# Attention scores of a two-layer transformer from two exact parts of q and k in the rounded four-byte type, one 32-row tile of TensorE per head, instead of three bf16 parts in 64-row tiles

## The reference

```python
q = jnp.einsum('bnc,hc->bnh', x, Wq).reshape(b, n, m, d)      # n = 1024, m = 16 heads, d = 8
k = jnp.einsum('bnc,hc->bnh', x, Wk).reshape(b, n, m, d)
v = jnp.einsum('bnc,hc->bnh', x, Wv).reshape(b, n, m, d)
scale = d ** (-0.25)
weight = jnp.einsum('bimd,bjmd->bmij', q * scale, k * scale)
weight = jax.nn.softmax(weight, axis=-1)
a = jnp.einsum('bmij,bjmd->bimd', weight, v).reshape(b, n, m * d)
return jnp.einsum('bnh,ch->bnc', a, Wout) + bout
```

## Time and profile before

| what | us | share of the span |
|---|---|---|
| median of three runs | 2011.02 | |
| profiled execution | 2013.06 | |
| its span | 2011.7 | |
| TensorE busy | 1826.9 | 91% |
| VectorE busy | 1521.9 | 76% |
| ScalarE busy | 1373.9 | 68% |
| GpSimd busy | 740.5 | 37% |
| weight loads of TensorE | 735.0 | 37% |
| DMA of hardware queue q1 | | 15.6% of 16 engines |

### The profile page before, as it was taken

The page is one execution under the profiler, slowest core; times in us unless marked ns, Lnnn a source line. Parts: engine busy times, 40 slices in busy tenths (PEclk is TensorE's granted clock), DMA queues, the critical chain, the costliest instruction groups (busy, mean ns, idle before and its releaser), DMA issues.

```text
span 2011.7 us, 39958 instructions
## 1 busy us (share of the span) xinstructions
PE 1826.9 (91%) x15950; PEld 735.0 (37%) x15950; DVE 1521.9 (76%) x2326; ACT 1373.9 (68%) x1826; POOL 740.5 (37%) x1150
## 2 busy tenths in 40 slices
PE   6675799999999999999999999999999999999994
PEld 4552333333433343343433344343433334222222
DVE  5456777888777877878777877778778787899961
ACT  2431467776687767777677766877677776887883
POOL 1441353315633265323744155332653145102001
PEclk9886799999999999999999999999999999999996
DMA  2012021012111121102211121111311021111101
GB/s 61 31 46 81 23 73 51 29 42 80 39 52 31 53 84 55 48 6 83 72 51 31 40 85 36 50 31 53 94 51 31 15 79 56 53 45 46 32 16 37
DMA packets 97258, 99.36 MB, mean 49 GB/s; under 512 B 11088, under 2 KB 81456, under 8 KB 97072
## 3 DMA queue, kind: packets, MB, share of 16 engines
q1 hardware_dynamic: 95224, 94.84, 15.6%
q10 hardware_dynamic: 1848, 1.97, 0.3%
HBM read 61.25 MB, written 34.73 MB: 48 GB/s over the span
## 4 chain that ended last, share of the span: by engine, by line
PE 63%; ACT 14%; DVE 11%; issue 5%; POOL 4%; DMA 1%; SPq 1%; ACTq 0%; POOLq 0%; DVEq 0%
PE pv_psum L667 18%; PE buffer L651 9%; PE buffer L641 9%; ACT p L846 9%; DVE row_max L1071 7%; PE side_psum L442 4%; PE side_psum L517 3%; PE side_psum L565 3%; PE side_psum L570 3%; PE side_psum L523 2%; PE side_psum L540 2%; PE side_psum L533 2%; PE side_psum L490 2%; PE side_psum L576 1%; POOL hm L1190 1%
## 5 line engine op out<-in xcount | busy, mean ns | idle before, releaser
L1071 DVE TENSOR_REDUCE row_max<-buffer 128x2 f32<-128x1024 f32 x1024 | 1239.6, 1221 | 319.5 <-PE buffer L641 305.9
L846 ACT ACTIVATE p<-buffer 128x1024 f32<-128x1024 f32 x1024 | 1044.0, 1025 | 283.5 <-PE buffer L651 265.0
L667 PE MATMUL pv_psum<-p,v 128*9 128x256 f32 x8192 | 638.6, 384 | 5.3 <-ACT o_sb L852 2.4
L641 PE MATMUL buffer<-k_ops,q_ops 48*128 48x512 bf16 x2048 | 398.8, 387 | 59.6 <-ACT p L846 23.1
L651 PE MATMUL buffer<-q_ops,k_ops 51*128 51x512 bf16 x2048 | 401.1, 388 | 18.7 <-DVE row_max L1071 15.3
L667 PEld LDWEIGHTS pv_psum<-p,v 128*9 128x9 f32 x8192 | 121.6, 88 | 350.4 <-issue 325.8
L651 PEld LDWEIGHTS buffer<-q_ops,k_ops 51*128 51x128 bf16 x2048 | 98.2, 93 | 343.5 <-DVE row_max L1071 155.6
L1203 POOL TENSOR_SCALAR nm_parts<-nm 128x16 bf16<-128x16 f32 x64 | 13.3, 208 | 413.2 <-DVE nm L1020 412.2
L641 PEld LDWEIGHTS buffer<-k_ops,q_ops 48*128 48x128 bf16 x2048 | 99.7, 94 | 178.9 <-ACT p L846 139.0
L1190 POOL TENSOR_TENSOR hm<-masks,hT_f 128x1024 f32<-128x1024 bf16 x64 | 136.6, 2146 | 39.5 <-PE side_psum L570 34.9
L1167 POOL TENSOR_TENSOR s<-s,consts 128x128 f32<-128x128 f32 x64 | 29.3, 458 | 242.5 <-ACT s L763 242.5
(11 more groups left out here) (245 smaller groups left out, 1873.5 us busy)
## 6 DMA issues: line engine op xcount, KB each, us to landing
masks<-masks_rows SPq DMA_DIRECT2D x16, 1024.0 KB, 5.6
q_ops<-products SPq DMA_DIRECT2D x128, 96.0 KB
k_ops<-products SPq DMA_DIRECT2D x124, 96.0 KB
products<-q_parts SPq DMA_DIRECT2D x16, 384.0 KB, 2.6
products<-k_parts SPq DMA_DIRECT2D x14, 384.0 KB, 2.9
attention<-o_sb SPq DMA_DIRECT2D x256, 18.0 KB
x<-in_L_attn_inputs SPq DMA_DIRECT2D x8, 512.0 KB, 4.0
products<-q_parts SPq DMA_DIRECT2D x16, 256.0 KB, 3.1
```

Source lines behind the costliest of these rows:

```text
L641: m = e.matmul(buffer[:, hh, :], q_ops[rows_of(hh, K_MAX), slot, of, i * P:(i + 1) * P], k_ops[rows_of(hh, K_MAX), slot, of, halves(half)[ ...
L667: m = e.matmul(pv_psum[q:q + VW, half * QUARTER:(half + 1) * QUARTER], v1[b % 2][:, kb, 2 * hp + hh, :], p_sb[n % 4][:, hh, part * QUARTER ...
L846: e.activation(p_sb[n % 4][:, :, :], unit("exp", n)[0][:, :, :], ACT.Exp).then_inc(S["exp_done"], 1)
L1071: e.tensor_reduce(mx[pair % 2][:, :, i, half], unit("max", n)[0][:, :, :], axis=AX.X, op=ALU.max).then_inc(S["max_done"], 1)
```

## The change

Two type and layout changes go together.

1. q, k and the maxima are split into **two** parts in float32r (`F32R`: four bytes, mantissa rounded) instead of three in bf16. Three products are stacked: 24 rows (`K_MAX`), 26 with the two parts of the maximum (`K_EXP`). All tiles and the DRAM buffer of the operands become float32. Score matmuls read them as float32r.
2. A head gets **32** rows of the array (`ROW_TILE`). The exp scores read partitions 0 to 63, the max scores partitions 64 to 127, so each half's four score matmuls lie in four different row tiles. The same rows are therefore fetched twice, once for `max` 43 halves ahead and once for `exp` 11 halves ahead, for one pair at a time, into two slots each.

With them go: ScalarE's copy of the first part (L802) and two of GpSimd's four instructions on the maxima; one of the three instructions of a split of q or k; a memset of `k_ops` of another shape; the transposition of the maxima in float32. The three bf16 parts of the experts' bias stay (`BE_PARTS`). The planner and its tables are not touched.

```diff
-PARTS = 3
-Q_PART = (0, 0, 0, 1, 1, 2)
-K_PART = (0, 1, 2, 0, 1, 0)
+BE_PARTS = 3
+PARTS = 2
+Q_PART = (0, 0, 1)
+K_PART = (0, 1, 0)
...
-ROW_HALF = 64
-GROUP = 2
-GROUPS = HEADS // 2 // GROUP
-SLOTS = 3
+ROW_TILE = 32
+SLOTS = 2
...
-    q_ops = sb("q_ops", [P, SLOTS, GROUP, N], BF16)
-    k_ops = sb("k_ops", [P, SLOTS, GROUP, N], BF16)
+    q_ops = sb("q_ops", [P, SLOTS, N])
+    k_ops = sb("k_ops", [P, SLOTS, N])
...
+    def fetch_operands(queue, kind, pair, w):
+        b, hp = divmod(pair, HEADS // 2)
+        for hh in range(2):
+            head = DH * (2 * hp + hh)
+            queue.dma_start((q_ops, k_ops)[w][rows_of(kind, hh, K_MAX), pair % SLOTS, :],
+                            products_dram[b % 2, w, :, head:head + DH, :]).then_inc(operands(kind, pair)[0], 16)
+
+    def rows_of(kind, hh, count):
+        first = ROW_TILE * (hh if kind == "exp" else 2 + hh)
+        return slice(first, first + count)
...
         def exp_scores(n):
...
+            pe.wait_ge(*operands("exp", pair))
             pe.wait_ge(*maxima_in(pair))
             for hh in range(2):
-                m = e.matmul(buffer[:, hh, :], k_ops[rows_of(hh, K_EXP), slot, of, kb * P:(kb + 1) * P],
-                             q_ops[rows_of(hh, K_EXP), slot, of, halves(half)[1]], start=True, stop=True)
+                m = e.matmul(buffer[:, hh, :], k_ops[rows_of("exp", hh, K_EXP), slot, kb * P:(kb + 1) * P].bitcast(F32R),
+                             q_ops[rows_of("exp", hh, K_EXP), slot, halves(half)[1]].bitcast(F32R), start=True, stop=True)
...
         def qk1(b, w, half):
             v, cols = filled("qk1", b, w, half), halves(half)[1]
-            act.wait_ge(S[f"parts{w}"], 16 * STORES * b)
-            e.copy(qk1_parts[w][:, 0, cols], v)
...
-        for hh in range(2):
-            e.memset(k_ops[ROW_HALF * hh + 32:ROW_HALF * (hh + 1), :, :, :], 1.0).then_inc(S["operands_set"], 1)
+        for slot in range(SLOTS):
+            e.memset(k_ops[0:2 * ROW_TILE, slot, :], 1.0).then_inc(S["operands_set"], 1)
...
-            after(e.tensor_tensor(r, r, p[:, 0, :], op=ALU.subtract))
-            after(e.tensor_scalar(p[:, 1, :], r, 1.0, 0.0, ALU.mult, ALU.add))
-            e.tensor_tensor(p[:, 2, :], r, p[:, 1, :], op=ALU.subtract).then_inc(S[f"split{w}_{half}"], 1)
+            pool.wait_ge(S[f"parts{w}"], 16 * STORES * b)
+            after(e.tensor_scalar(p[:, 0, :].bitcast(F32R), q, 1.0, 0.0, ALU.mult, ALU.add))
+            e.tensor_tensor(p[:, 1, :].bitcast(F32R), q, p[:, 0, :], op=ALU.subtract).then_inc(S[f"split{w}_{half}"], 1)
...
+        def load_operands(kind, pair):
+            sp.wait_ge(S["operands_set"], SLOTS)
+            if pair >= SLOTS:
+                sp.wait_ge(S[f"{kind}_filled"], UNITS * (pair - SLOTS + 1))
...
+            for kind, lead in (("max", 2 * LEAD), ("exp", 0)):
+                pair, within = divmod(h + lead + LOAD_BEFORE, UNITS)
+                if within == 0 and pair < PAIRS and (kind, pair) != ("max", 0) and pair >= 0:
+                    load_operands(kind, pair)
```

More of the change, by code:

```diff
@@ L6 @@
 BF16 = mybir.dt.bfloat16
+F32R = mybir.dt.float32r
 U32 = mybir.dt.uint32
@@ L336, in build @@
     mx = [sb(f"row_max{i}", [P, 2, T, HALVES]) for i in range(2)]
-    nm, nm_r = sb("nm", [P, 2, T]), sb("nm_r", [P, 2, T])
-    nm_parts = sb("nm_parts", [P, 2, PARTS, T], BF16)
-    nm_rows = [sb(f"nm_rows{i}", [PARTS * 2 * T, P], BF16) for i in range(2)]
+    nm = sb("nm", [P, 2, T])
+    nm_parts = sb("nm_parts", [P, 2, PARTS, T])
+    nm_rows = [sb(f"nm_rows{i}", [PARTS * 2 * T, P]) for i in range(2)]
     o_sb = sb("o_sb", [P, BANK])
@@ L384, in loaded, with operands @@
         return S[f"in_x{b % 4}"], 16 * (b // 4 + 1)
-    def operands(g):
-        return S[f"operands{g % SLOTS}"], 4 * GROUP * 16 * (g // SLOTS + 1)
+    def operands(kind, pair):
+        return S[f"{kind}_operands{pair % SLOTS}"], 4 * 16 * (pair // SLOTS + 1)
     def maxima_in(pair):
@@ L411, in store_parts @@
             queue.dma_start(dst, src).then_inc(S[f"parts{w}"], 16)
-    def fetch_operands(queue, g, w):
-        b, slot, p0 = g // GROUPS, g % SLOTS, (g % GROUPS) * GROUP
-        for of in range(GROUP):
-            for hh in range(2):
-                head = DH * (2 * (p0 + of) + hh)
-                queue.dma_start((q_ops, k_ops)[w][rows_of(hh, K_MAX), slot, of, :],
-                                products_dram[b % 2, w, :, head:head + DH, :]).then_inc(S[f"operands{slot}"], 16)
-    def rows_of(hh, count):
-        return slice(ROW_HALF * hh, ROW_HALF * hh + count)
+    def fetch_operands(queue, kind, pair, w):
[7 more added lines that the diff above has]
+        return slice(first, first + count)
     def tensor_program():
@@ L636, in max_scores @@
             pair, i, half = n // (2 * T), n // 2 % T, n % 2
-            slot, of = pair // GROUP % SLOTS, pair % GROUP
-            buffer = buffer_of("max", n)
-            pe.wait_ge(*operands(pair // GROUP))
+            slot, buffer = pair % SLOTS, buffer_of("max", n)
+            pe.wait_ge(*operands("max", pair))
             for hh in range(2):
-                m = e.matmul(buffer[:, hh, :], q_ops[rows_of(hh, K_MAX), slot, of, i * P:(i + 1) * P],
-                             k_ops[rows_of(hh, K_MAX), slot, of, halves(half)[1]], start=True, stop=True)
+                m = e.matmul(buffer[:, hh, :], q_ops[rows_of("max", hh, K_MAX), slot, i * P:(i + 1) * P].bitcast(F32R),
+                             k_ops[rows_of("max", hh, K_MAX), slot, halves(half)[1]].bitcast(F32R), start=True, stop=True)
             m.then_inc(S["max_filled"], 1)
@@ L1290, in sync_program @@
         sp.wait_ge(S["be_split"], 1)
-        for j in range(PARTS):
+        for j in range(BE_PARTS):
             e.dma_start(be3[j * EXPERTS:(j + 1) * EXPERTS, :], be_parts[:, j, :]).then_inc(S["be3_in"], 16)
@@ L1298, in parts @@
             if b >= 2:
-                for g in range((b - 1) * GROUPS - GROUPS, (b - 1) * GROUPS):
-                    sp.wait_ge(*operands(g))
+                for pair in range((b - 1) * HEADS // 2 - SLOTS, (b - 1) * HEADS // 2):
+                    sp.wait_ge(*operands("max", pair))
+                    sp.wait_ge(*operands("exp", pair))
             store_parts(e, b, w, half)
```

79 lines of the change are left out of this document (34 added, 45 removed).

## The result

The changed kernel takes 2087.74 us (median of four runs, 2081.48 to 2089.49) against 2011.05 (2006.14 to 2013.58) for the kernel before: ratio 1.0379, 95% interval 1.0350 to 1.0408, or 76 us more. The forecast was 1978, with a range up to 2045; the time lies outside it. The profiled execution took 2089.5 us, with a span of 2087.8, at a mean granted clock of 0.923; before it was 0.965.

The account below looks back on a forecast made before the run. Each half was taken as bound by TensorE's chain or, where it waits, ScalarE's exponential. 2013 - 70 (overlap) + 51 (weight loads) - 8 (casts) - 6 (start) = 1980, less 2 from profile to median: 1978 us, range 1915 to 2045.

Parts of the forecast that it names:

- The type's term: Float32r weight load exposed in each of 1024 halves, +50 ns over bf16: 51 us more, ends 0 and 105.
- The doubled loads: Operand loads on SP's queue double from 252 to 504 DMAs, hidden by a lead of 11 halves: costed at nothing.
- a wait of either scores for an operand DMA inside the loop: Sign that would refute costing the doubled operand loads at nothing.
- The overlap: Four score matmuls stream together, 0.215 us less in halves that don't wait: 70 us off of a 128 us ceiling.
- The rule of the waiting halves: Max scores start no earlier than 1.56 us after the previous exp scores, so waiting halves hand back their predecessor's saving.
- two cycles a column: Rival: float32r score matmuls stream at half rate, max scores to values 0.52 us; say 2140 us, chance 0.12.
- Waits for ScalarE: Max scores' waits for ScalarE's exponential rise from 398 and 139 us to some 550 times and over 250 us.
- The rest: ScalarE's casts of L802 gone, 8 us off; a shorter start, 6 us off; GpSimd, maxima and VectorE's memsets nothing.
- The load is the two-instruction one: Rival: float32r weight load costs 103 ns more instead of 50, 105 us in all; 2034 us, chance 0.12.
- No overlap: Rival: exp and max scores don't stream together, or the max scores' load cancels it; 2005 to 2020 us, chance 0.07.
- the f32 rate: Rival: score matmuls stream 512 columns in 0.95 us instead of 0.213; near 2680 us, chance 0.04.
- under 0.97 in the middle, since the array is then less busy than before: Sign: a granted clock this low in the middle of the loop would refute a term costed at nothing.

Follow-up runs that it names:

- loads_apart: The changed kernel with the exp scores' operand loads issued 15 halves ahead instead of 11: 2046.94 us, ratio 1.0180 to the kernel before.
- apart_stacked: loads_apart with both kinds of scores reading the same 56 rows per head, in two 64-row tiles instead of four: 2080.58 us, ratio 1.0340.
- bf16_apart_stacked: bf16_apart with both kinds of scores reading the same 56 rows per head, in two 64-row tiles instead of four: 1989.64 us, ratio 0.9878.
- The fillers: Zero-weight bf16 matmuls behind the values of halves without side stage, added to the changed kernel (2078.28 us) and to loads_apart (2045.29 us).
- bf16_tiles: The changed kernel with its two parts in bf16 instead of float32r, for operands, parts and maxima: 1965.24 us, ratio 0.9772.
- bf16_apart: bf16_tiles with the exp scores' operand loads issued 15 halves ahead instead of 11: 1956.43 us, ratio 0.9734.

## Why the prediction was wrong

Its sum was 2013 - 70 + 51 - 8 - 6 + 0, less 2 us between profile and median. By the table the same terms are -32, +92, -25 and +40 us. Two steps failed, the load's size and the queue at nothing, and a third thing had no term at all: the time at the lower clock.

**The type's term, 51 us: about 92.** The load was taken as that of a transposition, 50 ns over bf16. It reads 189 and 193 ns in the profile after, 96 to 100 over the bf16 loads of the earlier trace rows, and changing the type alone costs 90 and 93 us. In the halves at full clock in both traces of a pair that is 84 ns a half with four tiles and 90 with two. The step that failed is "I take the one-instruction four-byte load". The prediction's own mark was "93 or 196 moves the sum by 51 us down or 54 up", and it read nearly 196. The Trainium skill's rule that was cited (TensorE: Matmul & The Clock Gate, section Weight-path perf modes) has the fast load for types other than FP32 and doesn't place float32r; the trace places it with FP32, 189 and 193 ns against 196 for f32 and 91 to 94 for bf16. Counting it once for each half was right: 0.11 us more per half whether or not it waits.

**The doubled loads, 0 us: 40.** The failing step is "I cost it at nothing; what hides it is the lead of 11 halves". The lead was compared with one transfer, while what mattered was the small DMA of the maxima behind eight loads in the same queue. The lead did hold for the operands, since no score waits for a `products` load inside the loop, but seven times it did not for the maxima. The listed mark, "a wait of either scores for an operand DMA inside the loop", came true. That the maxima are "needed 10 and more halves later" was wrong already for the kernel before: once in a sequence they stood some 9 us in SP's queue and landed less than 1 us ahead of use, and its view of the waits shows two such waits, 1.3 us in all. Nor does "each of the same size" make two loads equal: the traces show about six of sixteen DMA engines at work for loads before and about three after. In the loop the 39 us are 16 us of waits and 22 us of lower clock behind them, net of what loads_apart has elsewhere. With half the bytes all is worth 8.

**The overlap, 70 us off: 32.** That four tiles stream together is shown: 429 of the 898 halves at full clock have their max scores less than 0.02 us behind the exp scores. The rule of the waiting halves was also right in size. In halves at full clock in both traces of a pair, the four tiles take 69 us off with float32r (967 halves) and 61 with bf16 (952). Where it comes from differs by type. With bf16, exp to max scores loses 68 us and max scores to values gains 8. With float32r it is 136 and 71: with a common start the second load has no stream to hide behind, so 0.11 us moves from one interval to the other. What was missing is the clock: loads_apart has 104 us at the low level in the loop against 14 in apart_stacked, and 30 us of the 69 are lost there; with bf16 it is 126 against 18, and 31 of the 61. The marks of the prediction read accordingly: exp to max scores under 0.03 held; max scores to values of 0.31 to 0.36 holds for bf16 (0.31 where undelayed) and not for float32r (0.42 to 0.43); 0.52, two cycles a column, is refuted.

**Waits for ScalarE** were to rise from 398 and 139 us to 550 and over 250. They fell to 291 and 113.8; a longer TensorE half leaves ScalarE more time, which is argued and not tested alone. With bf16 and the loads apart, four tiles instead of two make the matching figures 389 times and 171 us against 389 and 141, and the waits booked on the matmuls themselves 171 and 57 against 80 and 22: the argument was right in direction for a load that costs little.

**The rest, 14 us off: 25.** Casts, start, VectorE and ScalarE work, and one product part fewer. In the traces of the kernel before and bf16_apart_stacked it is 15 us in the loop, nearly all between the values and the next exp scores, and 8 us ahead of the first exp scores. The loop was costed at 8 us. The start isn't resolved by one profile: the first max scores stood at 169.4 us before and at 153.8 to 167.4 in the profiles of the kernels with two parts, and two of them with the same code for the start differ by 6.7 us. In the changed kernel the store of the k parts took 7.87 us and the first operands 7.78, against 6.35 and 6.91 in the earlier trace rows, and the first max scores came 2 us earlier than before, not 6.

**The rivals.** "The load is the two-instruction one" had 2034 us and named the right load. The 54 us between it and the measured time are the overlap (+38), the loads in the queue (+40), the rest (-11), and a type's term of 92 instead of 105 (-13). No rival had the queue or the clock. No overlap, two cycles a column and the f32 rate are refuted.

**The clock.** The mark "under 0.97 in the middle, since the array is then less busy than before" came true in part (0.98 and 0.91 in the first two stretches of the earlier trace rows), but it had no price in the sum. The price is 55 us of the change's 74 in the loop (section on the result), 0.33 us for each microsecond at the low level, in halves that were at full clock before. It isn't a fifth term beside the four of the table: each of them is measured with its share of it, above all the tiles (30 us) and the queue (22 us). At full clock throughout, the change would have cost some 20 us, an estimate: 76 less 55. The fillers agree: they gain 0.28 and 0.31 us for each microsecond that they lift to full clock, and lose 21 and 24 us by their own work. Two things stay open. Why the kernel with four row tiles falls to the low level in loads_apart, where no DMA wait starts it, no run shows. And a lower clock doesn't decide alone: bf16_tiles has 142 us of it in the loop, more than the 104 of loads_apart, and is 82 us faster.

**The better version.** bf16_apart, at 0.9734, beats both kernels, at the price of scores with fewer bits than float32. With float32r, the loads apart are the better form of the change, but still 1.8% slower than before.

## What to carry to other kernels

Before a type is changed, ask what its weight load costs and whether that load is exposed: here 100 ns on a load outweighed a stream that vanished, since an overlap that merges two starts also exposes the second load, and since the four tiles came with more time at the lower clock. Where loads are split or doubled, look for the smallest and latest DMA behind them in the same queue and compare the lead with its landing, not with theirs; a short wait of that kind in the trace before, here 1.3 us, says that the lead is used up. A gain in one interval of a loop is measured over the whole loop, by the sum of every interval; here 150 us became 32. To price a lower clock, compare the same halves at both levels in two traces; halves with different work mislead.

## What the runs showed of the hardware

- Float32r matmuls stream 512 columns in nearly the time of bf16: with the second load hidden (apart_stacked) max scores to values is 0.32 us against 0.31, and with it exposed 0.42 against 0.31, about the difference of the loads. By the Trainium skill, page FP8 and Floating Point Precision, section TensorE Precision Notes, true FP32 takes four passes through the array, while a reduced-precision FP32 is read as four bytes and truncated; the trace agrees with one pass for it.
- A float32r load of 128 columns takes 0.18 us at full clock and 0.28 at 1.2 GHz, for 24, 26 and for 56 rows nearly alike (189 and 193, 183 and 187 ns in the mean), where bf16 takes 91 to 94.
- Four row tiles on four PSUM banks start within 0.01 us of each other, for both types.
- 8 KB behind eight loads of 96 KB landed 8.87 us after its issue. While such loads, and at most stores of parts beside them, were under way, 0.38 of the sixteen DMA engines were busy with six products along the load's first dimension and 0.19 with three.
- After 3.93 us of idle time in the loop, TensorE stayed at the 1.2 GHz level for 68 us although the profile has it busy without a gap; with filler matmuls the same wait was followed by 10 us of it, and with two row tiles instead of four a wait of 4.06 us by 7.
- The same 34 halves took 65.8 us at 1.2 GHz and 47.0 at full clock: 1.4 times as long, not twice.
